# Gather ahead of the low parts, no loads for a turn that does not come, and four stores

## The reference, cut to what matters

```python
topk_idx, topk_w = _route(x, router_w, e_bias)          # 8 of 64 experts for each of 800 tokens
coef = zeros((T, E)).at[arange(T)[:, None], topk_idx].add(topk_w)
g = einsum('th,ehi->tei', x, Wg)
u = einsum('th,ehi->tei', x, Wu)
h = silu(g) * u * coef[:, :, None]
moe_out = einsum('tei,eih->th', h, Wd)
shared = silu(x @ SWg) * (x @ SWu) @ SWd
return moe_out + shared
```

## Time and profile before

| what | value |
|---|---|
| time, median of 3 runs | 668.62 us (666.63 to 671.85) |
| the profiled execution's own time | 669.29 us |
| its span | 667.6 us |
| mean granted TensorE clock | 0.97 |
| PE busy | 613.9 us (92%) |
| DVE, ACT, POOL busy | 382.5, 403.2, 304.9 us |

### The profile page before, as it was taken

How to read it: one execution, slowest core, us unless ns; L and a number is a source line. 1 busy time by engine, 2 the same in 40 slices (tenths; PEclk the granted TensorE clock), 3 DMA queues, 4 the chain that set the end, 5 groups by cost and what they waited for, 6 DMA issues and landing times.

```text
span 667.6 us, 15448 instructions
## 1 busy us (share of the span) xinstructions
PE 613.9 (92%) x4792; PEld 498.3 (75%) x4793; DVE 382.5 (57%) x1205; ACT 403.2 (60%) x973; POOL 304.9 (46%) x486
## 2 busy tenths in 40 slices
PE   8999899999989999898999999999897899999992
PEld 7998566666668899876887666666665899999991
DVE  2543677777751111158989746665684666666661
ACT  4555899898844343245666787868452555555551
POOL 4214555558564000021010005777235788888880
PEclk9999999999969999999999999999988899999996
DMA  6139600007245993012210010000026877776774
GB/s 160 51 99 318 216 2 3 1 2 245 59 140 168 302 322 115 32 53 62 52 35 1 10 45 1 2 1 1 7 92 141 233 186 198 185 189 171 196 197 124
DMA packets 75192, 73.80 MB, mean 111 GB/s; under 512 B 10976, under 2 KB 68350, under 8 KB 75010
## 3 DMA queue, kind: packets, MB, share of 16 engines
q1 hardware_dynamic: 66792, 62.22, 30.7%
q0 software_dynamic: 4816, 8.07, 5.9%
q10 hardware_dynamic: 3530, 2.82, 1.6%
HBM read 57.78 MB, written 15.31 MB: 109 GB/s over the span
## 4 chain that ended last, share of the span: by engine, by line
PE 60%; ACT 11%; issue 7%; DVE 7%; DMA 6%; SPq 4%; POOL 3%; DVEq 0%; POOLq 0%; ACTq 0%
PE psum L1388 5%; PE psum L1399 5%; ACT probs L911 4%; PE psum L1890 3%; PE psum L1912 3%; PE psum L1899 3%; PE psum L1938 2%; PE psum L837 2%; PE psum L827 2%; DMA x_rows<-xc_dram,slot_rows 2%; PE psum L2333 2%; PE psum L1673 1%; POOL probs L977 1%; PE psum L1677 1%; PE psum L1674 1%
## 5 line engine op out<-in xcount | busy, mean ns | idle before, releaser
L911 ACT ACTIVATE probs<-probs,negmax 100x361 f32<-100x361 f32 x128 | 68.9, 587 | 10.6 <-POOL probs L977 10.5
L990 DVE TENSOR_SCALAR_CACHE_REDUCE probs<-psum 100x361 f32<-100x361 f32 x128 | 60.7, 531 | 17.2 <-PE psum L827 17.2
L837 PEld LDWEIGHTS psum<-ident,probs 100*128 100x128 f32 (+1 forms) x384 | 38.0, 151 | 25.2 <-issue 16.7
L837 PE MATMUL psum<-ident,probs 100*128 100x100 f32 (+1 forms) x384 | 45.9, 256 | 10.8 <-ACT probsT L919 4.0
L977 POOL TENSOR_SCALAR probs<-probs 100x722 f32<-100x722 f32 x64 | 50.5, 789 | 5.1
L1429 ACT ACTIVATE kT_all<-psum,kT_all 128x128 f32<-128x128 f32 x88 | 25.2, 369 | 42.8 <-PE psum L1388 42.8
L2538 PE MATMUL psum<-xT_high,we_high 128*128 128x400 f32 x128 | 45.7, 357 | 5.1 <-POOL we_low L2713 3.1
L2539 PE MATMUL psum<-xT_low,we_high 128*128 128x400 f32 x128 | 45.4, 355 | 0.0
L2540 PE MATMUL psum<-xT_high,we_low 128*128 128x400 f32 x128 | 45.3, 354 | 0.0
L1388 PE MATMUL psum<-kT_all,v_all 128*128 128x128 f32 x352 | 41.4, 276 | 3.7 <-issue 3.7
L1388 PEld LDWEIGHTS psum<-kT_all,v_all 128*128 128x128 f32 x352 | 40.7, 192 | 5.4 <-issue 5.0
(11 more groups left out here) (471 smaller groups left out, 1789.9 us busy)
## 6 DMA issues: line engine op xcount, KB each, us to landing
v_all<-in_L_ffn_W_dram SPq DMA_DIRECT2D x16, 1024.0 KB, 7.5
xs_dram<-zeros SPq DMA_DIRECT2D x1, 7424.0 KB, 23.7
kT_all<-coefT_dram SPq DMA_DIRECT2D x18, 400.0 KB, 4.4
v_all<-in_L_ffn_Wg_dram SPq DMA_DIRECT2D x36, 128.0 KB, 2.9
v_all<-in_L_ffn_Wu_dram SPq DMA_DIRECT2D x36, 128.0 KB, 3.0
v_all<-in_L_ffn_Wd_dram SPq DMA_DIRECT2D x36, 128.0 KB, 3.5
ctx_nat<-in_ctx_dram SPq DMA_DIRECT2D x16, 192.0 KB, 2.4
rank_rows<-rank_dram SPq DMA_DIRECT2D x18, 100.0 KB, 3.5
```

Of the source, the lines that this page charges most:

```text
L837: last = nc.tensor.transpose(pT_ps[0:rows[t], t, hh * NQ:(hh + 1) * NQ], probs[:, n % NPB, hh, t * P:t * P + rows[t]], ident[0:NQ, 0:NQ])
L911: last = nc.scalar.activation(row, row, ACT.Exp, bias=negmax[:, n % NPB, hh:hh + 1])
L990: last = nc.vector.tensor_scalar(probs[:, n % NPB, hh, 0:NKV], psum[0:NQ, n % 2 * 2 + hh, 0:NKV], -CLAMP, None, ALU.max, ALU.max, accum_ou ...
```

## The change

- In `pe_attend1` five products of zeros stand in the place of three, ahead of the last batch's transposes.
- In `pe_shared` the first down product of the shared expert moves from ahead of the counting of the picks to behind the making of the list, and six products of zeros are added at its end, behind a wait for `route_taken`.
- SP loads gate and up of dense expert 1 of turn 0 behind the first coefficient row and not ahead of it.
- In the loop SP loads for turn i + 1 only where there is such a turn. Before, the last turn also loaded a set that nobody used; ACT's first step for it still waits for `we_loaded`, so that SP raises this semaphore itself behind the loop. The final waits for the unused loads go, on SP and on ACT.
- POOL's `gather(i)` goes ahead of the two low parts of the down weights.
- The output is stored in four pieces of two batches and not in two of four.

```diff
--- before.py
+++ after.py
@@ -1967,7 +1967,7 @@
             pe_transpose_x1(pe, b)
         for b in range(B - 2):
             pe_logits1(pe, b)
-        for _ in range(3):
+        for _ in range(5):
             nc.tensor.matmul(psum[:, 5, 0:D], zeros[:, 0:P], zeros[:, :], start=True, stop=True)
 
     def act_attend1(act):
@@ -2268,9 +2268,9 @@
         sp.wait_ge(ranks_stored, 16)
         for k in range(2):
             load_rank(k, small_at(sp, total, 0, k))
-        load_gate_up(1, dense[1])
         sp.wait_ge(coefT_stored, 16)
         load_coef(0, 0, dense[0])
+        load_gate_up(1, dense[1])
         load_down(1, dense[1])
         load_small(0, 0, small_at(sp, total, 0, 0))
         load_coef(0, 1, dense[1])
@@ -2279,7 +2279,7 @@
             with sp.If(2 * PAIRS * o < total):
                 with sp.Fori(0, PAIRS) as j:
                     i = o * PAIRS + j
-                    with sp.If(2 * i < total):
+                    with sp.If(2 * i + 2 < total):
                         dense = [load(i + 1, p) for p in range(2)]
                         load_coef(i + 1, 0, dense[0])
                         load_small(i + 1, 0, small_at(sp, total, i + 1, 0))
@@ -2287,12 +2287,12 @@
                             load_rank(k, small_at(sp, total, i + 1, k))
                         load_small(i + 1, 1, small_at(sp, total, i + 1, 1))
                         load_coef(i + 1, 1, dense[1])
+        for p in range(2):
+            sp.wait_ge(we_loaded[p], 16 * total)
+            sp.sem_inc(we_loaded[p], 32)
         for k in range(2):
             sp.wait_ge(rows_added[k], 8 * total)
         sp.dma_start(x[:, 1:B + 1, :], sum_dram[0:B * NQ, :].rearrange("(b q) d -> q b d", b=B)).then_inc(x_loaded[0], 16)
-        for p in range(2):
-            sp.wait_ge(coef_loaded[p], 8 * total + 16)
-            sp.wait_ge(rank_loaded[p], 8 * total + 16)
         sp.wait_ge(rows_added[0], 8 * total + 16)
 
     def pe_router_transposes(pe):
@@ -2340,7 +2340,6 @@
                 nc.tensor.matmul(yT_ps[2 * half + c], swd[:, m, c * P:(c + 1) * P],
                                  sh_hT[:, m, half * HT:(half + 1) * HT], start=(m == 0), stop=False)
 
-        down(0, 0)
         pe.wait_ge(sh_taken, 5)
         pe.wait_ge(route_step, 1)
         pe.wait_ge(consts_ready, N_SPARSE)
@@ -2371,6 +2370,7 @@
         rank_picks(1, 5, B)
         pe.wait_ge(route_step, 2)
         nc.tensor.matmul(r_list_ps, e_col, place[:, :], start=True, stop=True).then_inc(route_sums, 1)
+        down(0, 0)
         pe.sem_inc(gu_in_psum, 8)
         pe.sem_inc(y1_in_psum, 8)
         for k in range(2):
@@ -2384,6 +2384,9 @@
         down(0, 1)
         for half in range(2):
             down(1, half)
+        pe.wait_ge(route_taken, 2)
+        for _ in range(6):
+            nc.tensor.matmul(psum[:, 3, 0:D], zeros[:, 0:P], zeros[:, :], start=True, stop=True)
 
     def act_take_router(act):
         act.wait_ge(router_step, R_WT_IN_PSUM)
@@ -2696,10 +2699,6 @@
                             take_hidden(i, k)
                         for k in range(2):
                             take_small(i, k)
-        for k in range(2):
-            act.wait_ge(ws_loaded[k], 24 * total + 48)
-        for p in range(2):
-            act.wait_ge(wd_loaded[p], 8 * total + 16)
         for half in range(2):
             for c in range(2):
                 act.wait_ge(experts_done, 2 * half + c + 1)
@@ -2771,9 +2770,9 @@
                 with pool.Fori(0, PAIRS) as j:
                     i = o * PAIRS + j
                     with pool.If(2 * i < total):
+                        gather(i)
                         for p in range(2):
                             split(i, p, 1, slice(WGU, WALL))
-                        gather(i)
                         for half in range(2):
                             hidden(i, 0, half)
                         add_second(i)
@@ -2883,12 +2882,12 @@
             sp_project1(sp)
             sp_load_ffn1(sp)
             sp_experts1(sp)
-            for k in range(2):
-                sp.wait_ge(x_final, 2 * k + 2)
-                half = slice(k * B // 2, (k + 1) * B // 2)
-                sp.dma_start(a["out"][half].rearrange("b q d -> q b d"), x[:, 1 + half.start:1 + half.stop, :]
+            for k in range(4):
+                sp.wait_ge(x_final, k + 1)
+                two = slice(2 * k, 2 * k + 2)
+                sp.dma_start(a["out"][two].rearrange("b q d -> q b d"), x[:, 1 + two.start:1 + two.stop, :]
                              ).then_inc(out_stored, 16)
-            sp.wait_ge(out_stored, 32)
+            sp.wait_ge(out_stored, 64)
 
         @block.gpsimd
         def _(pool):
```

## The result

| | before | after |
|---|---|---|
| time, median of 4 runs (lowest to highest) | 668.79 us (666.63 to 671.85) | 677.25 us (675.12 to 678.41) |
| ratio to before | 1 | 1.0119, 95% interval 1.0085 to 1.0153 |
| profiled execution: time, span | 669.29, 667.6 us | 676.37, 674.8 us |

The forecast was 676.5 us, range 666 to 680.5. The changed kernel is 1.2% slower.

What follows compares the result with a forecast made beforehand. PE, busy 92% of the span, was taken as the bound, with waits in the expert stage. Span 667.6 + 8.3 (longer turns, less end savings) - 0.4 (stores) = 675.5 us; time 676.5 against the median, range 666 to 680.5.

Steps and rivals of the forecast that it cites:

- The ring: Expert turns: row_of, gathers, low part, SP's loads, rank rows, compares, next row_of; 18.66 us a turn against 16.92.
- Rival A: Expert turns: low parts and rank rows keep their time, all gains stand; 660 to 662 us, chance 0.12.
- B: Expert turns: a light ring of about 17.7 us from shorter landing and gathers; about 670 to 671 us, chance 0.18.
- C: Expert turns: a heavy ring of 19.3 us from slow landing and held-up gathers; 680 us, chance 0.08.
- every L2801 from turn 2 on waits for the rank rows: Sign of a right forecast: DVE's compare stands for the rank rows in each turn from turn 2; no size given.
- L2752 starts right behind L2804: Sign of a right forecast: POOL goes on to the gather as soon as DVE has made row_of; no size given.
- The work on POOL stays the same; its order changes: POOL, expert turns: the gather starts about 1.75 us sooner with unchanged work; gain 2.5 us at most.
- Slack and landing: Expert turns: the earlier gather removes the wait for the rows, 2.5 us; DVE's 1.36 us slack covers one late turn.
- The end: Last turn to output: add at 654.8, x asked for at 660.0, x and PE's transposes even, span 675.5 us.
- The term for the ninth turn's loads: SP, last turn: useless loads delay reading x back by 2.8 us; removed waits cost and save nothing.
- The router: Shared expert and routing: moving the down product ends DVE's wait for the counts; gain 0.4 us.
- Products of zeros: PE, before the last transposes and after the shared expert: little or no cost, possible clock gain in turn 0; counted 0.

Runs made afterwards that it cites:

- gather_only: The kernel before with only POOL's gather moved ahead of the two low parts of the down weights; 681.09 us, ratio 1.018.
- gather_back: The changed kernel with the gather put back behind the two low parts of the down weights; 664.93 us, ratio 0.9916.
- ranks_late: The changed kernel with SP loading the rank rows behind small expert 1's weights as well; 692.95 us, ratio 1.0353.
- ranks_mid: The changed kernel with SP loading the rank rows ahead of small expert 0 and not behind it; 670.60 us, ratio 1.0031.
- gather_mid: The changed kernel with the gather between the two low parts of the down weights; 675.32 us, ratio 1.0105.
- ranks_first: The changed kernel with SP loading the rank rows ahead of the dense experts' weights, behind a wait for row_of; 670.51 us, ratio 1.0004.
- back_loads: gather_back with the unused loads for a ninth turn and the old final waits kept; 669.00 us, ratio 1.0016.
- order_back: The changed kernel with expert 1's gate and up of turn 0 loaded ahead of the first coefficient row again; 676.64 us, ratio 1.0109.
- first_back: ranks_first with the gather put back behind the two low parts of the down weights; 665.39 us, ratio 0.9941.
- back_order_zeros: back_order with both edits of the products of zeros undone; 660.78 us, ratio 0.9901.
- mid_low_later: gather_mid with DVE's second ws_low moved behind the next half of the hidden product; 661.31 us, ratio 0.9911.
- back_order: The changed kernel with the edits of both gather_back and order_back; 661.88 us, ratio 0.9914.

## Why the prediction was right, step by step

**The ring.** Forecast 18.66 us, measured 18.70. `row_of` of turn 1 was forecast at 535.1 and is made at 534.5, that of turn 7 at 647.1 and 646.7. `gather_only` shows that the move makes the loss, `gather_back` that nothing else does, `ranks_late` that the ring's length counts. Rival A (no ring), B (17.7) and C (19.3) fell as descriptions of after. The weight load's waits in L2541 and L2563, 9.8 us in the 140 us from 520 to 660 or 1.3 a turn, are of the size forecast for PE's idle time. But that 18.66 meets 18.70 so closely is luck. Of the signs, "every L2801 from turn 2 on waits for the rank rows" and "L2752 starts right behind L2804" held only in every second turn. The ring on its own shows in `ranks_late`, where POOL waits for `row_of` in all turns: its ordinary turns of 20.4 to 20.7 less the 2.25 added put the ring of after at 18.1 to 18.5 us, by estimate. The rest of the 18.70 is DVE and POOL, in the turns between.

**Its terms** were less good than their sum. In turn 3 the gathers and the pause took 2.32 us, not 2.88, which was the lower bound of 2.33; `row_of` to the first gather took 0.94, not 0.45; low part to load 1.67, not 1.46; landing and signal 3.71, not 4.0; SP's 7.57 was 7.67. The errors cancel: -0.56 - 0.29 + 0.49 + 0.21 + 0.10 = -0.05. The Trainium skill's rule on the ports, by which the gather drops to 1.05 us (page "SBUF — State Buffer", section "Who interferes with whom"), was right on this term: the first gather takes 1.02 or 1.03 us in turns 1 to 7. The prediction's doubt was right too. In turns 2, 4 and 6 the second gather takes 1.62 us, beside DVE's first `ws_low`; in the others it takes 0.98. The sum of 18.1 drawn from the rule was not what the turns take, as other terms grew.

**"The work on POOL stays the same; its order changes"** was the sentence that failed: it put the price of the new order at nothing. The order decides which instruction of POOL runs beside which of DVE. The order also decides when POOL's later work is done. Both give a pace of their own, just under the ring: POOL's late `h_low` one of 17.4 to 17.8 us, the held `ws_low` one of 18.45. The first is why loosening the ring in `ranks_mid` regains only 1.2 of the 2.06 us between after and `gather_back`. The second is why opening it in `gather_mid` regains 0.25. In after itself the `ws_low` of turns 1, 3, 5 and 7 take 1.5 and 2.9 to 3.0 us, and the first gather is 0.6 us shorter than in before. Even without the ring the turns would not have been rival A's: `ranks_first` has none, and 17.73 us.

**Slack and landing.** The rows' wait of 2.5 us is gone, as forecast, and worth nothing in after.

**The end.** Forecast: add at 654.8, x asked for at 660.0, x and PE even at 667.7 and 668.0, span 675.5. Measured: 655.2, 659.1, PE last at 667.04 + 1.95 = 669.0, span 674.8. The term for the ninth turn's loads was 2.8 us, plus 0.4 for the stores; `back_loads` shows 5.6 for the loads and waits where turns are short. The term was mis-sized because it took the add's landing as the median of 5.1 us, with the loads gone as with them. Without them it is 3.8 us, so that x is asked for 3.9 us behind the add and not 5.2. Against this the add itself came 8.5 us behind `row_of` and not 7.7, and little of the gain is seen in after, since there PE is last.

**The router.** Gain forecast 0.4, measured 0. PE timelines of after, first router product to the products that follow the list:

```profile
482.27 10.97 PE L2333 MATMUL psum<-kT_all,stage_arena 128*128 128x400 f32 x32
...
498.11 0.27 PE L2372 MATMUL psum<-v_all,iota 64*1 64x64 f32 x2 [1.03 <-DVE v_all L2507]
```

15.84 us. In `gather_only`, which has the old order, it is the same (484.11 to 499.95). In before it is 16.63 us, from 484.54 to 501.17, because L2333 took 12.66 us and not 10.97; from 484.70 to 488.10 us its granted clock was 0.52, where that of after and `gather_only` was 1.00. The line of before:

```profile
484.54 12.66 PE L2333 MATMUL psum<-kT_all,stage_arena 128*128 128x400 f32 x32
```

The 0.8 us in favour of after is thus the clock, not the place of the down product.

**Products of zeros.** Counted as 0, and 0 they are. PE stands 0.54 us before its first expert product, not 3.08, yet it stands longer a little later, and the clock falls then. PE's next product after 512.09 in after, and the window 515.70 to 522.50 (columns as in the earlier trace rows):

```profile
518.33 0.70 PE L2541 MATMUL psum<-xT_high,we_high 128*128 128x400 f32 x1 [5.90 <-DVE v_all L2794]
```

```profile
515.70:522.50 6.80, 4.17 (x13) 4.13 (x14) 4.80 (x7) 4.49 (x9) 5.47 (x7) 0.51 0.51 159
```

0.51 is the half speed of 1.2 GHz. The stand comes from expert 1's gate and up. SP issues the up weights at 508.90 us, and ACT, waiting for them, starts its high part 5.75 us later. The page has 2.4 us as this load's median to landing. Here many loads are under way at once: the window 512.00 to 515.40 has a DMA share of 1.13 and 318 GB/s. That this is the reason was not tested; `order_back` says that its place does not set the time.

**What stays open.** The cause of the 17.27 us of `first_back`; and how much of after's 2.06 us is ring and how much is held-up DVE, since the chain takes them by turns and either alone leaves most of the time lost.

**A better version.** `back_order_zeros` (0.9901), `mid_low_later` (0.9911), `back_order` (0.9914) and `gather_back` (0.9916) beat both kernels and cannot be told apart. All keep the skipped loads and four stores, and in none does the first low part stand behind the wait for `row_of`.

## What to carry to other kernels

Before work is moved behind a wait, follow what its end releases on other queues, and add up that path back to the wait: if the sum exceeds the turn, every turn pays the difference, however much idle time each engine shows. The same move also changes which VectorE and GpSimd instructions overlap, so compare their durations line by line (min, median, max) before and after. When a sum of terms meets the measured turn, look at several turns all the same: here every second one was paced by something else. Loads that nobody uses are not free at the end of a loop: the read that ends the kernel stands in the same queue, and the transfer that it waits for lands later beside them.

## What the runs showed of the hardware

- A VectorE instruction with two operands in SBUF can be held for longer than one GpSimd instruction: `ws_low`, 0.95 us alone, took 2.93 to 3.38 us beside two or three low parts of GpSimd in a row, and ended 0.81 to 0.83 us behind the last of them in the turns shown (after and `gather_mid`). The Trainium skill, page "SBUF — State Buffer", section "Who interferes with whom", calls the shared port pair an exclusive lock and says, of VectorE's 2-port modes, that whoever issues first has it for the whole instruction and the other blocks. The collisions agree with it, as that rest is about the length of a `ws_low` alone; that the one who waits can stand behind several instructions in a row is what these rows add.
- Even an instruction of 0.23 us that reads and writes two columns (L2804, a tensor_scalar) took 1.93 to 1.97 us beside GpSimd's low parts, in four turns of `first_back`.
- The indirect DMA that adds rows in HBM landed in 5.1 to 5.7 us where SP's loads went on beside it, and in 3.8 to 4.5 us where they did not (the last turn's `add_second`, three and eleven kernels).
- Two kernels that differ only in where VectorE's second `ws_low` stands, at the same amount of work on every engine, are 2% apart (1.0105 and 0.9911).
